# Edge weights of a relational attention layer: 8 or 9 of 12 or 13 tile products moved from VectorE to GpSimd, diagonal products on TensorE replaced by rows of ones

## The reference, cut to what matters

```python
z = h @ W
s_src = z @ attn[:d]
s_dst = z @ attn[d:]
e = leaky_relu(s_src[src] + s_dst[dst])
m = segment_max(e, dst)
ex = exp(e - m[dst])
denom = segment_sum(ex, dst)
alpha = ex / denom[dst]
coef = rel_table[etype, 0] * alpha
out = segment_sum(coef[:, None] * z[src], dst)
```

## Time and profile before

| | us |
|---|---|
| three runs: median (lowest to highest) | 3380.41 (3377.36 to 3380.56) |
| the profiled execution's own time | 3380.8 |
| its span from the first to the last instruction | 3379.1 |
| first exponents to the last product of the stage, in the profile | 2764.4 to 3024.1 |
| VectorE / TensorE / ScalarE / GpSimd busy over the span | 2597.0 / 2511.1 / 1489.4 / 1952.3 |

### The profile page before, as it was taken

How to read it: one execution, slowest core, us unless ns; L and a number is a source line. 1 busy time by engine, 2 the same in 40 slices (tenths; PEclk the granted TensorE clock), 3 DMA queues, 4 the chain that set the end, 5 groups by cost and what they waited for, 6 DMA issues and landing times. The chain is left out here.

```text
span 3379.1 us, 87741 instructions
## 1 busy us (share of the span) xinstructions
PE 2511.1 (74%) x20390; PEld 1974.6 (58%) x20391; DVE 2597.0 (77%) x8325; ACT 1489.4 (44%) x3942; POOL 1952.3 (58%) x2344
## 2 busy tenths in 40 slices
PE   1433555555555554999999999999999239989899
PEld 1322334333334343999999999999997214445455
DVE  7863777777777773999999999999997779983501
ACT  2011222222222222677777777777775655452200
POOL 1005777777777777899999999999996000000000
PEclk9975677677777776999999999999999559999999
DMA  9993222222222223888888888888886669869766
GB/s 381 414 414 129 78 78 83 78 78 78 77 79 78 78 68 104 236 240 234 242 239 235 240 239 234 242 238 236 241 239 226 255 282 343 301 219 315 249 220 208
DMA packets 738172, 696.84 MB, mean 206 GB/s; under 512 B 48524, under 2 KB 637275, under 8 KB 734779
## 3 DMA queue, kind: packets, MB, share of 16 engines
q1 hardware_dynamic: 516770, 536.77, 47.6%
q10 hardware_dynamic: 195544, 104.71, 12.7%
q0 software_dynamic: 25792, 54.52, 4.9%
HBM read 340.91 MB, written 354.90 MB: 206 GB/s over the span
## 5 line engine op out<-in xcount | busy, mean ns | idle before, releaser
L855 POOL DMA_INDIRECT sorted_rows<-rows,posi x806 | 785.1, 974 | 338.7 <-issue 221.4
L1147 DVE SCALAR_TENSOR_TENSOR acc<-acc,keep,pm 128x256 f32<-128x256 f32 x1504 | 715.7, 476 | 70.9 <-issue 23.9
L965 POOL TENSOR_SCALAR ohs_e<-iota,rt 128x128 f32<-128x128 f32 x1128 | 666.2, 607 | 12.4 <-DMA rt<-sorted_rows 12.4
L803 PE MATMUL s_peq<-sb_w1bb,eT 128*128 128x256 f32 x806 | 352.5, 531 | 398.9 <-ACT eT L658 379.9
L1074 PE MATMUL pm<-ohw_e,ohs_e 128*128 128x128 f32 x3008 | 609.1, 283 | 0.0
L974 POOL TENSOR_TENSOR hid<-pre_e,excess 128x512 f32<-128x512 f32 x376 | 482.8, 1284 | 117.2 <-ACT excess L1001 117.2
L1080 PE MATMUL px<-PN,dT 128*128 x4512 | 498.1, 219 | 0.4 <-ACT dT L1014 0.4
L1020 ACT ACTIVATE ohw_e<-ohd_e,rt 128x128 f32<-128x128 bf16 x1504 | 490.5, 397 | 0.0
L1074 PEld LDWEIGHTS pm<-ohw_e,ohs_e 128*128 128x128 f32 x3008 | 461.8, 194 | 0.0
L803 PEld LDWEIGHTS s_peq<-sb_w1bb,eT 128*128 128x128 f32 x806 | 172.8, 265 | 441.1 <-ACT eT L658 432.7
L1091 PE MATMUL ps<-hid,ohs_e 128*128 128x129 f32 x3008 | 424.3, 283 | 0.5 <-POOL hid L974 0.5
(11 more groups left out here) (317 smaller groups left out, 4206.3 us busy)
## 6 DMA issues: line engine op xcount, KB each, us to landing
count_matrices<-acc SPq DMA_DIRECT2D x1504, 128.0 KB, 2.6
sorted_rows<-zrow SPq DMA_DIRECT2D x188, 528.0 KB, 10.5
rt<-sorted_rows ACTq DMA_DIRECT2D x184, 528.0 KB, 4.6
gab<-count_matrices SPq DMA_DIRECT2D x60, 1280.0 KB, 6.0
arb<-count_matrices SPq DMA_DIRECT2D x25, 1664.0 KB, 8.8
ab<-count_matrices SPq DMA_DIRECT2D x25, 1600.0 KB, 9.3
arb<-count_matrices SPq DMA_DIRECT2D x25, 1536.0 KB, 8.5
ef<-in_edge_attr_dram SPq DMA_DIRECT2D x58, 364.0 KB
```

What stands on the lines that cost most here:

```text
L803: nc.tensor.matmul(pe_q[:, q % 2, 0:2 * D], eT[:, q % 2, :], w1bb[:], start=True, stop=True).then_inc(s_q, 1)
L855: pool.indirect_dma_start(sortd, bass.IndirectOffsetOnAxis(ap=posi[:, h, c:c + 1], axis=0), rows[:, h, c, :], None).then_inc(s_sc[h], 16)
L965: last = nc.gpsimd.tensor_scalar(ohs[:, k % BUFS, j, :], iota128[:], rt[:, k, j, D + 1:D + 2], None, ALU.is_equal)
L1147: nc.vector.scalar_tensor_tensor(acc[:, k % SUMS, j, :], before, keep[:, at:at + 1] if isinstance(at, int) else keep[:, ds(at, 1)], pm[:, ...
```

## The change

- VectorE's `tmp2` product is now for the last four tiles alone (`r:n`, `DV = 4`); the product for the other 8 or 9 tiles is a plain `tensor_tensor` multiply on GpSimd, `edge_weights(k)`, in a new block of that engine.
- GpSimd has no min in it, so the capped pair of Relu and Exp on ScalarE is now on those 8 or 9 tiles, and the plain Exp on the last four.
- TensorE makes no diagonal products. Rows of ones go over all 12 or 13 tiles, four tiles (512 columns) a row, behind the products with `H` instead of ahead of them. They have a bank of their own in each half.
- VectorE's `diagonals` is gone; `denominators` copies four tiles at a time.
- `zb`, a row of zeros, is a part of `DN` now.

```diff
-                DT = 4
-                ROWT = [b - a - DT for a, b in HALF]
+                DV = 4
+                ROWT = [b - a - DV for a, b in HALF]
-                DIAG = (NB, 0)
-                DROW = ((NB - 1, P), (1, 0))
-                RW = 3 * P
+                DROW = (NB, 0)
+                RW = BANK
...
                         if k >= LOADS:
                             sp.wait_ge(s_wt, 2 * (k - LOADS) + 2)
-                            sp.wait_ge(s_dg, k - LOADS + 1)
+                            sp.wait_ge(s_pm, k - LOADS + 1)
...
-                        nc.scalar.activation(e[:, r:n, :], e[:, r:n, :], ACT.Relu, bias=ss[:, 4, s:s + 1],
+                        nc.scalar.activation(e[:, 0:r, :], e[:, 0:r, :], ACT.Relu, bias=ss[:, 4, s:s + 1],
                                              scale=-1.0).then_inc(s_e, 1)
-                        nc.scalar.activation(e[:, 0:r, :], e[:, 0:r, :], ACT.Exp, bias=ss[:, 1, s:s + 1]).then_inc(s_e, 1)
+                        nc.scalar.activation(e[:, r:n, :], e[:, r:n, :], ACT.Exp, bias=ss[:, 1, s:s + 1]).then_inc(s_e, 1)
                         act.wait_ge(s_e, 3 * k + 2)
-                        nc.scalar.activation(e[:, r:n, :], e[:, r:n, :], ACT.Exp, scale=-1.0).then_inc(s_e, 1)
+                        nc.scalar.activation(e[:, 0:r, :], e[:, 0:r, :], ACT.Exp, scale=-1.0).then_inc(s_e, 1)
...
                         if k >= 3:
-                            dve.wait_ge(s_mm, k - 2)
+                            dve.wait_ge(s_pm, k - 2)
+                            dve.wait_ge(s_wt, 2 * k - 4)
                         nc.vector.scalar_tensor_tensor(ex[:, k % 3, 0:b - a, :], RBv[:, 0, a:b, :], ss[:, 3, s:s + 1],
                                                        RBv[:, 1, a:b, :], ALU.add, ALU.max).then_inc(s_t, 1)
...
-                        nc.vector.scalar_tensor_tensor(tmp2[:, k % 2, 0:r, :], ex[:, k % 3, 0:r, :], 2.0, arb[:, k % LOADS, 0, 0:r, :],
+                        nc.vector.scalar_tensor_tensor(tmp2[:, k % 2, r:n, :], ex[:, k % 3, r:n, :], 2.0, arb[:, k % LOADS, 0, r:n, :],
                                                        ALU.min, ALU.mult).then_inc(s_wt, 1)
...
-                        if k == NT + 3:
-                            diagonals(0)
...
-                    diagonals(1)
...
+                @block.gpsimd
+                def _(pool):
+                    def edge_weights(k):
+                        h, s = STEPS[k]
+                        r = ROWT[h]
+                        pool.wait_ge(s_e, 3 * k + 3)
+                        pool.wait_ge(s_ld[k % LOADS], 16 * (k // LOADS + 1))
+                        if k >= 2:
+                            pool.wait_ge(s_mm, k - 1)
+                        nc.gpsimd.tensor_tensor(tmp2[:, k % 2, 0:r, :], ex[:, k % 3, 0:r, :], arb[:, k % LOADS, 0, 0:r, :],
+                                                ALU.mult).then_inc(s_pm, 1)
+
+                    for k in range(len(STEPS)):
+                        edge_weights(k)
...
-                        for j in range(DT):
-                            last = nc.tensor.matmul(num[:, DIAG[h], j * P:(j + 1) * P], ex[:, k % 3, r + j, :], arb[:, k % LOADS, 0, r + j, :],
-                                                    start=False, stop=final, skip_group_check=True)
-                        last.then_inc(s_dg, 1)
-                        bank, o = DROW[h]
-                        pe.wait_ge(s_wt, 2 * k + 1)
-                        flat = tmp2[:, k % 2, :, :].rearrange("p q d -> p (q d)")
-                        for g in range(-(-r // 3)):
-                            w = min(RW, r * P - g * RW)
-                            nc.tensor.matmul(num[32 * g:32 * g + 1, bank, o:o + w], ones[:, 0:1], flat[:, g * RW:g * RW + w],
-                                             start=False, stop=final, skip_group_check=True)
...
+                        pe.wait_ge(s_pm, k + 1)
+                        flat = tmp2[:, k % 2, :, :].rearrange("p q d -> p (q d)")
+                        for g in range(-(-n // 4)):
+                            w = min(RW, n * P - g * RW)
+                            last = nc.tensor.matmul(num[32 * g:32 * g + 1, DROW[h], 0:w], ones[:, 0:1], flat[:, g * RW:g * RW + w],
+                                                    start=False, stop=final, skip_group_check=True)
                         last.then_inc(s_mm, 1)
...
                         if k == NT:
-                            pe.wait_ge(s_ev, 3)
+                            pe.wait_ge(s_ev, 2)
                             clear(0)
-                            clear(1)
```

More of the change, by code:

```diff
@@ L1610, in build @@
                 rx = sb("rx", [P, 2, 13, P])
-                tmp2 = sb("tmp2", [P, 2, max(ROWT), P])
+                tmp2 = sb("tmp2", [P, 2, 13, P])
                 H2 = sb("H2", [P, HALF[0][1], D])
-                zb = sb("zb", [1, BANK])
-                dgm = sb("dgm", [P, DT, P])
+                zb = DN[0:1, 1, :]
                 dens = sb("dens", [P, NT])
@@ L1622, in build @@
                 s_wt = sem("w_edge_and_relation_weights")
-                s_dg = sem("w_diagonal_products")
+                s_pm = sem("w_edge_weights_by_pool")
                 s_mm = sem("w_products")
@@ L1664, in exp @@
                         act.wait_ge(s_t, k + 1)
-                        nc.scalar.activation(e[:, r:n, :], e[:, r:n, :], ACT.Relu, bias=ss[:, 4, s:s + 1],
+                        nc.scalar.activation(e[:, 0:r, :], e[:, 0:r, :], ACT.Relu, bias=ss[:, 4, s:s + 1],
                                              scale=-1.0).then_inc(s_e, 1)
-                        nc.scalar.activation(e[:, 0:r, :], e[:, 0:r, :], ACT.Exp, bias=ss[:, 1, s:s + 1]).then_inc(s_e, 1)
+                        nc.scalar.activation(e[:, r:n, :], e[:, r:n, :], ACT.Exp, bias=ss[:, 1, s:s + 1]).then_inc(s_e, 1)
                         act.wait_ge(s_e, 3 * k + 2)
-                        nc.scalar.activation(e[:, r:n, :], e[:, r:n, :], ACT.Exp, scale=-1.0).then_inc(s_e, 1)
+                        nc.scalar.activation(e[:, 0:r, :], e[:, 0:r, :], ACT.Exp, scale=-1.0).then_inc(s_e, 1)
                     def evacuate(h):
-                        bank, o = DROW[h]
                         act.wait_ge(s_mm, NT * (h + 1))
-                        nc.scalar.activation(DN[:, h, 0:RW], num[:, bank, o:o + RW], ACT.Copy).then_inc(s_ev, 1)
+                        nc.scalar.activation(DN[:, h, 0:RW], num[:, DROW[h], :], ACT.Copy).then_inc(s_ev, 1)
                         for c in GROUPS[h]:
@@ L1735, in weights @@
                                                        ALU.min, ALU.mult).then_inc(s_wt, 1)
[L1737 to L1742, removed]
                     def denominators(h):
@@ L1746, in denominators @@
                         dve.wait_ge(s_tr, h + 1)
-                        for g in range(-(-ROWT[h] // 3)):
-                            n = min(3, ROWT[h] - 3 * g)
-                            last = nc.vector.tensor_copy(dens[:, a + 3 * g:a + 3 * g + n],
+                        for g in range(-(-(b - a) // 4)):
+                            n = min(4, b - a - 4 * g)
+                            last = nc.vector.tensor_copy(dens[:, a + 4 * g:a + 4 * g + n],
                                                          num[:, 2, 0:n * P].rearrange("p (q d) -> p q d", d=P)[:, :, 32 * g])
@@ L1777, in scales @@
                                                        ALU.mult, ALU.mult).then_inc(s_nb, 1)
-                    nc.vector.memset(zb[:], 0.0).then_inc(s_z, 1)
+                    nc.vector.memset(zb, 0.0).then_inc(s_z, 1)
                     exponent(0)
@@ L1811, in clear @@
                     def clear(bank):
-                        nc.tensor.matmul(num[:, bank, :], ones[0:1, :], zb[:], start=True, stop=False, skip_group_check=True)
+                        nc.tensor.matmul(num[:, bank, :], ones[0:1, :], zb, start=True, stop=False, skip_group_check=True)
                     def products(k):
@@ L1816, in products @@
                         a, b = HALF[h]
-                        n, r = b - a, ROWT[h]
+                        n = b - a
                         final = s == NT - 1
-                        pe.wait_ge(s_e, 3 * k + 3)
-                        pe.wait_ge(s_ld[k % LOADS], 16 * (k // LOADS + 1))
-                        for j in range(DT):
-                            last = nc.tensor.matmul(num[:, DIAG[h], j * P:(j + 1) * P], ex[:, k % 3, r + j, :], arb[:, k % LOADS, 0, r + j, :],
-                                                    start=False, stop=final, skip_group_check=True)
-                        last.then_inc(s_dg, 1)
-                        bank, o = DROW[h]
-                        pe.wait_ge(s_wt, 2 * k + 1)
-                        flat = tmp2[:, k % 2, :, :].rearrange("p q d -> p (q d)")
-                        for g in range(-(-r // 3)):
-                            w = min(RW, r * P - g * RW)
```

(14 more changed lines are left out.)

## The result

The changed kernel takes 3448.42 us (median of 4 runs, 3448.27 to 3451.23) against 3378.89 of the kernel before on the same chip: a ratio of 1.021, 95% interval 1.0194 to 1.0226, 69.5 us slower. 3458 was forecast, in a range from 3400 to 3510. The profiled execution took 3451.23 us, its span is 3449.5, 70.4 more than before.

What follows compares the result with a forecast made beforehand. The prediction took VectorE to bound the stage, with TensorE and the loads close behind. Terms 94.5 - 7.0 - 6.0 - 2.75 + 0.4 - 2 = +77 us on 3380.8 gave 3458 us, range 3400 to 3510.

Steps and rivals of the forecast that it cites:

- The mechanism: In the stage's steps, GpSimd's SBUF-reading multiply holds VectorE's two-SBUF-input instructions, so a step costs the sum; chance 0.70.
- rival (a): In the stage's steps, VectorE and GpSimd run side by side: -38 us, 3343 us; chance 0.15.
- the 324 pairs: On edges, 324 of 327 L1169 on VectorE that start during GpSimd's L974 end 0.07 to 0.12 us behind it.
- The hold in half 0: GpSimd's 2.35 us multiply less 0.14 us of overlap, added to VectorE's own 4.01 us step.
- The multiply itself: GpSimd's product of exponents and counts: 2.35 us for 1024 columns, 2.62 for 1152, middle of two bounds.
- half 1: 1.96 more, times 25: Half 1's step goes from 4.93 to 4.27 + 2.62 = 6.89 us; 25 steps give +49.0 us.
- the overlap: In both halves, 0.14 us of each GpSimd multiply lies beside VectorE's work: 50 x 0.14 = -7.0 us.
- The 6.0 us stop: VectorE's wait between the halves for half 1's first products; forecast to go, -6.0 us.
- TensorE has no backlog: At the stage's end VectorE's 4.7 us wait shrinks to 1 to 4 us: -2 us.
- Rival (c): In the stage, TensorE falls to its lower clock and bounds: +156 us, 3537 us; chance 0.07, shared with a worse queue.
- Rival (b): In the stage's steps, VectorE is held for only half the multiply: +22 us, 3403 us; chance 0.08.

## Why the prediction was right, and where its sum was off

**The mechanism** was read from the right rows. The earlier trace rows showed VectorE held behind L974, and the changed loop does the same in every step. The run with memsets shows that neither the waits, nor the order on TensorE, nor GpSimd's writes lengthen the step, and the run with a row in PSUM shows that the exponents are held only when both of their rows lie in SBUF. Ahead of the change the evidence was thin, as the prediction itself says under rival (a): the 324 pairs are of L1169, which reads one tensor (`iota`) and a column of scalars, so they show that L974 can hold VectorE, but can't speak for a rule on two inputs. For that there was one pair, L1127's. The hold in half 0 was forecast as 2.35 - 0.14 = 2.21 us and is 6.13 - 4.01 = 2.12. The multiply itself was forecast as 2.35 us, the middle between two bounds, 2.13 and 2.57; that it came out at 2.36 is in part luck.

The Trainium skill (SBUF — State Buffer, sections SBUF: two separate sides and Who interferes with whom) says that a VectorE instruction with two SBUF inputs contends with a GpSimd instruction that reads SBUF, and that the loser blocks for the whole instruction. The trace agrees with the first part. For the second it shows 2.12 us of 2.36 for the multiply of 1024 columns, and with one input on GpSimd 2.71 of 3.13 for 1152 columns, but 0.78 of 2.77 for 1024; the measurement decides.

**The sum** by places, from the starts of the `rx` products (first, 25th, 50th: 2771.53, 2880.46, 3017.51 before, 2770.35, 2919.76, 3085.63 after) and the ends of the spans:

| | forecast | measured |
|---|---|---|
| up to the first `rx`, one step | 1.82 - 0.14 = 1.7 | -1.2 |
| the next 24 steps, half 0 | 24 x 1.68 = 40.3 | 40.5 |
| the next 25 steps, half 1 | 25 x 1.82 - 6.0 - 1.4 = 38.1 | 28.8 |
| behind the last `rx` | -1.4 + 0.4 - 2 = -3.0 | +2.3 |
| all | 77 | 70.4 |

The sum came out only 7 us too high because its misses partly cancel, -9.3 in half 1 against +5.3 behind it. The first two lines belong together, since the first step's multiply holds the first `rx` and so comes behind its start: 39.3 measured against 42.0, of which 25 x (2.21 - 2.12) = 2.3 are the hold. The term that was most mis-sized is "half 1: 1.96 more, times 25" (1.82 with the overlap). A regular step there is 6.63 and 6.72 us by turns, 6.67, so 1.74 more and not 1.82. The last step has no exponents to hold, and got 0.5 us shorter; it must not be in the 25. And the update of half 0 lies among these steps: while VectorE does that, GpSimd's multiply can run beside it and holds less.

```profile
2989.89 0.34 DVE L1750 SCALAR_TENSOR_TENSOR X<-num,rden,X 128x128 f32<-128x128 f32 x1
2989.95 2.62 POOL L1806 TENSOR_TENSOR tmp<-ex,arb 128x1152 f32<-128x1152 f32 x1 [4.92 <-ACT ex L1667]
2990.26 0.87 DVE L1755 BATCH_NORM_STATS2 stats<-X 128x6 f32<-128x128 f32 x4
2991.16 3.16 DVE L1719 SCALAR_TENSOR_TENSOR ex<-RB,ss 128x1664 f32<-128x1664 f32 x1
```

Here 2.62 us of GpSimd (just the forecast length) cost the exponents 1.2 and not 2.4. With 24 x 1.74 - 0.5 - 6.0 - 1.4 = 33.9, some 5 us are left to the 28.8 measured, and such places account for them: the 24 intervals from the 25th to the 49th `rx` are 134.0 us before, 15.7 more than 24 steps of 4.93, and 163.3 after, some 3 more than 24 of 6.67. Of the 15.7 the stop is 6.0 and the diagonals 1.4, so the update cost some 8 us before and some 3 after. The 6.0 us stop did go: VectorE shows no idle time between the halves.

The second mis-sized term is the end: "TensorE has no backlog". It has, because the last step of VectorE, without exponents, is only 2.6 us long:

```profile
3085.63 1.89 DVE L1732 SCALAR_TENSOR_TENSOR rx<-ex,arb 128x1664 f32<-128x1664 f32 x1
...
3087.95 1.03 PE L1832 MATMUL num<-tmp,ones 128*1 128x512 f32 x8
3088.91 3.06 PE L1826 MATMUL num<-rx,H 128*128 128x512 f32 x8
3091.91 1.03 PE L1832 MATMUL num<-tmp,ones 128*1 128x512 f32 x8
```

From the end of the last `rx`, 3087.5, to the end of the last row of ones, 3092.9, are 5.4 us, in place of the 4.7 of the earlier trace rows. VectorE's own stop there is longer still, 6.8 us, since it now waits for the turned rows of denominators as well, where it began with the diagonals before:

```profile
DVE dens L1740 <- PE num L1841: 6.8, 1, 6.8
```

It was forecast to get 2 us shorter and got 2.1 longer: 4.1 of the 5.3 us between -3.0 and +2.3.

**Rival (c)** came in part and did not set the pace: some steps' products take 4.3 to 4.8 us where others take 2.84 (half 0) and 3.06 (half 1), and the granted clock is 0.90 and 0.91 where the earlier trace rows had 0.95 and 1.00. But TensorE's step stays under VectorE's: in the windows above it is busy for 72% of the time and VectorE for 99% or more. Rival (b), half the multiply, fits no run with two inputs on GpSimd.

## What to carry to other kernels

Before work goes from VectorE to an idle GpSimd, look where the inputs of VectorE's neighbours lie: in these runs a VectorE instruction with two SBUF inputs and a two-input multiply on GpSimd take turns, and at about 2.05 ns against 1.03 ns a column every column moved lengthens the pair. An engine that is held shows as busy, so compare the duration of an unchanged instruction before and after, not the busy share. Where one operand of this operation lay in PSUM, or GpSimd only wrote, the two did run side by side. That is no rule for every operation with one SBUF input: L1169 of the earlier trace rows, a `tensor_scalar`, reads one tensor and was held all the same, and why was not tried.

## What the runs showed of the hardware that was not expected

A GpSimd `tensor_scalar` of 1024 columns took 2.77 us, longer than the two-input multiply (2.36), and held VectorE for only 0.78 of them; one of 1152 columns took 3.13 and held it for 2.71. Three memsets of the same tile, 2.9 us of GpSimd writes, held it for nothing.
